# Four scheduling edits in a two-layer transformer kernel: weight loads in parts, a shared gate ring, turned steps, paced clears

## The reference, cut to what matters

```python
def body(acc, p):                       # 64 routed experts, hidden width 64 each
    W1, B1, W2, B2, e = p
    h = jax.nn.silu(xf @ W1 + B1) @ W2 + B2
    cw = jnp.sum(jnp.where(ti == e, tw, 0.0), axis=-1)
    return (acc + cw[:, None] * h, None)
...
x = x + _L0_xattn_ref(_layernorm(x), ctx, ...)
x = x + _L0_ffn_ref(_layernorm(x), ...)           # routed + shared experts
x = x + _L1_xattn_ref(_layernorm(x), ctx, ctx, mask, ...)
x = x + _L1_ffn_ref(_layernorm(x), ...)           # h = gelu(x @ bw1.T + b1) @ bw2.T + b2
```

## Time and profile before

| | us |
|---|---|
| median of 3 runs | 1317.81 (1317.72 to 1319.56) |
| profiled execution | 1319.14 |
| its span, first to last instruction | 1317.4 |
| TensorE busy | 1167.9 (89%) |
| VectorE busy | 879.4 (67%) |
| ScalarE busy | 697.0 (53%) |
| GpSimd busy | 337.8 (26%) |
| mean granted TensorE clock | 0.953 |

### The profile page before, as it was taken

How to read it: one execution, slowest core, us unless ns; L and a number is a source line. 1 busy time by engine, 2 the same in 40 slices (tenths; PEclk the granted TensorE clock), 3 DMA queues, 4 the chain that set the end, 5 groups by cost and what they waited for, 6 DMA issues and landing times. The chain is left out here.

```text
span 1317.4 us, 20464 instructions
## 1 busy us (share of the span) xinstructions
PE 1167.9 (89%) x6928; PEld 1014.4 (77%) x6928; DVE 879.4 (67%) x1669; ACT 697.0 (53%) x1053; POOL 337.8 (26%) x347
## 2 busy tenths in 40 slices
PE   3888769988879979969999999999999999978988
PEld 2666647877768969969999988778788788767877
DVE  6787765556645635635665454799999989976565
ACT  2222214655533424424444233798888988976655
POOL 2400018212123500410320025432342432332020
PEclk9888879988889989989999999999999999998999
DMA  8100001002217253252222013322421423310001
GB/s 294 64 0 0 0 8 64 1 5 68 61 48 157 65 152 96 73 144 92 93 96 89 1 40 97 102 66 73 128 64 52 139 70 103 88 38 6 14 21 48
DMA packets 66852, 92.83 MB, mean 70 GB/s; under 512 B 15440, under 2 KB 32592, under 8 KB 66640
## 3 DMA queue, kind: packets, MB, share of 16 engines
q1 hardware_dynamic: 65152, 89.67, 23.1%
q10 hardware_dynamic: 1616, 2.10, 0.5%
HBM read 80.45 MB, written 11.14 MB: 70 GB/s over the span
## 5 line engine op out<-in xcount | busy, mean ns | idle before, releaser
L1823 DVE CUSTOM_DVE_ANT_0 at_pr<-at_sc,at_mk 128x512 f32<-128x512 f32 x256 | 165.5, 684 | 24.8 <-PE at_sc L2054 24.3
L1725 ACT ACTIVATE at_pr<-at_pr,at_nmx 128x512 f32<-128x512 f32 x256 | 170.4, 716 | 21.4 <-DVE at_nmx L1823 20.7
L1969 DVE TENSOR_TENSOR W_1l<-at_pt,W_1h 128x1024 fp32r<-128x1024 f32 x128 | 155.8, 1217 | 5.5 <-ACT W_1h L1720 5.2
L2069 PE MATMUL at_pt<-ident,at_pr 128*128 128x128 f32 x1024 | 135.9, 276 | 21.1 <-DVE W_1l L1969 20.4
L2069 PEld LDWEIGHTS at_pt<-ident,at_pr 128*128 128x128 f32 x1024 | 115.5, 142 | 44.5 <-issue 25.2
L1720 ACT ACTIVATE W_1h<-at_pt 128x1024 fp32r<-128x1024 f32 x128 | 130.8, 1022 | 34.5 <-PE at_o L2088 33.1
L315 DVE TENSOR_TENSOR moe_ms<-moe_hs,moe_gate 128x512 f32<-128x512 f32 x112 | 86.2, 770 | 89.9 <-ACT moe_hs L282 56.6
L282 ACT ACTIVATE moe_hs<-moe_hid,cols 128x512 f32<-128x512 f32 x128 | 88.1, 688 | 104.0 <-PE moe_hid L167 103.0
L274 ACT ACTIVATE moe_hh<-moe_ms 128x512 fp32r<-128x512 f32 x112 | 70.8, 632 | 133.4 <-DVE moe_ms L315 133.4
L301 DVE TENSOR_TENSOR moe_hl<-moe_ms,moe_hh 128x512 fp32r<-128x512 f32 x112 | 87.9, 785 | 69.2 <-ACT moe_hh L274 69.2
L2088 PE MATMUL at_o<-W_1h,at_vaug 128*128 128x512 f32 x256 | 113.7, 444 | 0.3 <-DVE W_1l L1969 0.3
(11 more groups left out here) (314 smaller groups left out, 3293.6 us busy)
## 6 DMA issues: line engine op xcount, KB each, us to landing
moe_gate<-expert_weights SPq DMA_DIRECT2D x224, 128.0 KB, 2.9
w_stage<-in_ew SPq DMA_DIRECT2D x8, 1024.0 KB, 6.3
at_kp<-at_heads SPq DMA_DIRECT2D x96, 64.0 KB, 2.7
at_qp<-at_heads SPq DMA_DIRECT2D x96, 64.0 KB, 2.8
w_stage<-in_w SPq DMA_DIRECT2D x4, 1024.0 KB, 9.8
f_gate<-expert_weights SPq DMA_DIRECT2D x32, 128.0 KB, 2.9
w_stage<-in_mask SPq DMA_DIRECT2D x16, 256.0 KB, 3.6
at_rb<-at_recip SPq DMA_DIRECT2D x64, 64.0 KB, 2.0
```

What stands on the lines that cost most here:

```text
L1725: act.activation(pr_of(t)[:, x, :], pr_of(t)[:, x, :], ACT.Exp, bias=nmx[:, t % 4, x:x + 1], scale=-1.0).then_inc(s["ex"], 1)
L1823: dve.tensor_tensor_reduce(pr_of(t)[:, x, :], SB[x][:, :], mk[u // 2 % 2][:, j, :], -float(HD) ** -0.5, 3.0e38, ALU.add, ALU.min, nmx[:, t ...
L1969: dve.tensor_tensor(PH[1][:, n % 2, :], PT[n % 2][:, :, :].rearrange("p c q -> p (c q)"), f(PH[0][:, n % 2, :]), ALU.subtract).then_inc(s[ ...
L2069: last = pe.transpose(PT[t % 2][:, c, j * P:(j + 1) * P], pr_of(t - i + j // 2)[:, j % 2, kc * P:(kc + 1) * P], g.ident[:, :])
```

## The change

Four parts.

1. `group_dma` loads each group in eight parts of 256 KB. In `moe_phase` they are set between the gates: for q = 0 in the batch i = 3, one part behind the gates of each tile; for q = 1 and 2 in the batches i = 2 and 3, one part behind the gates of every second tile. SP's loop is written out.
2. The gate ring and its semaphores are allocated outside `front_phase` and `moe_phase` and used by both. `front_phase` issues the gates of the first four tiles of batch 2 at its end, and `moe_phase` leaves those out.
3. Last unit: TensorE's turns go to steps 3, 4, 6, 7 (they were in 3, 4, 7, 8). ScalarE's copies and VectorE's low parts of them go to steps 4, 5, 7, 8, ScalarE's ahead of L1720 and the exponentials of the step. `alphas` and `alphas2` stand behind L1969 of steps 10 and 12, not ahead.
4. GpSimd in the preparation: each pair of the clears of QP waits for one low part of the tail (`tlo`), `low_ctx` stands behind the second pair, and the clears of VAUG go in four parts, each behind a later low part and followed by one conversion of the mask.

```diff
-def group_dma(sp, g, k):
-    if k:
+PARTS = 8
+def group_dma(sp, g, k, parts=range(PARTS)):
+    if k and 0 in parts:
         sp.wait_ge(g.w_split, SPLITS * k)
...
+    for part in parts:
+        c, half = divmod(part % 4, 2)
+        if part < 4:
+            n = slice(half * H // 2, (half + 1) * H // 2)
+            sp.dma_start(first[:, c, n], g.a[name1][c * P:(c + 1) * P, at + n.start:at + n.stop]).then_inc(g.w_staged, 16)
+        else:
+            t = 2 * (part - 4)
+            sp.dma_start(second[:, t:t + 2, :],
+                         g.a[name2][at + t * P:at + (t + 2) * P, :].rearrange("(t p) n -> p t n", p=P)).then_inc(g.w_staged, 16)
 def group_split(pool, g, k):
-    pool.wait_ge(g.w_staged, 32 * (k + 1))
+    pool.wait_ge(g.w_staged, 16 * PARTS * (k + 1))
...
 # front_phase, SP, behind the last store of the expert weights
+            gates(EARLY, RING)
...
 # moe_phase, SP
             for q in range(GR):
-                first = 0 if q else EARLY
-                gates(q, first)
-                if q + 3 < GR + 2:
-                    group_dma(sp, g, q + 3)
-                with sp.Fori(first + 1, B) as i:
-                    gates(q, i)
+                for i in range(0 if q else EARLY, B):
+                    for t in range(HT):
+                        if q or i > EARLY or t >= RING:
+                            gates(q, i, t)
+                        if q + 3 < GR + 2:
+                            if q == 0 and i == B - 1:
+                                group_dma(sp, g, q + 3, range(t, t + 1))
+                            elif q and i >= B - 2 and t % 2:
+                                part = (i - B + 2) * HT // 2 + t // 2
+                                group_dma(sp, g, q + 3, range(part, part + 1))
...
 # attention_phase, GpSimd
             norm_pool(pool, nm, 0, g.power)
-            low_ctx(0)
-            clear(QP[:, :, :].rearrange("p a n -> p (a n)"), T)
+            for k in range(4):
+                pool.wait_ge(s["tlo"], k + 1)
+                clear(heads[:, 2 * k * T:2 * (k + 1) * T], T)
+                if k == 1:
+                    low_ctx(0)
             add_bias(0)
-            clear(VAUG[:, :, :, :, :].rearrange("p s t g w -> p (s t g w)"), 3 * PERIOD)
+            for k in range(4):
+                pool.wait_ge(s["tlo"], k + 6)
+                clear(places[:, 6 * PERIOD * k:6 * PERIOD * (k + 1)], 3 * PERIOD)
+                convert(0, k)
             ones()
-            for j in range(TT):
-                convert(0, j)
...
 # attention_phase, ScalarE: ahead of the copy L1720 of the step
+                    if u == UNITS - 1 and st in (4, 5, 7, 8):
+                        ffn_turn(st - 4 if st < 7 else st - 5)
...
-                    if u == UNITS - 1 and st in (3, 4, 7, 8):
-                        ffn_turn(st - 3 if st < 7 else st - 5)
...
 # VectorE
+                        if st in (4, 5, 7, 8):
+                            ffn_low_turn(st - 4 if st < 7 else st - 5)
                         if st in (2, 5):
                             ffn_apply(st // 3)
-                        if st in (3, 4, 7, 8):
-                            ffn_low_turn(st - 3 if st < 7 else st - 5)
...
 # TensorE
-                        if st in (3, 4, 7, 8):
-                            ffn_turn(st - 3 if st < 7 else st - 5)
+                        if st in (3, 4, 6, 7):
+                            ffn_turn(st - 3 if st < 6 else st - 4)
```

More of the change, by code:

```diff
@@ L189, in __init__ @@
         if gated:
-            self.gate = sb(name + "_gate", [P, RING, T], F32)
             self.ms = sb(name + "_ms", [P, RING, T], F32)
-            self.gate_loaded = [sem(f"{name}_gate_loaded{i}") for i in range(RING)]
             self.gate_used = sem(name + "_gated")
@@ L417, in build @@
                 g.cw = nc.dram_tensor("expert_weights", (E, B * T), F32).ap()
[L418 to L421 removed]
+                g.gate_loaded = [sem(f"gate_loaded{k}") for k in range(RING)]
+                with ExitStack() as st2:
+                    g.gate = maker(st2)[0]("gate", [P, RING, T], F32)
+                    with ExitStack() as st3, own_semaphores():
+                        front_phase(nc, g, *maker(st3))
+                    with ExitStack() as st3, own_semaphores():
+                        moe_phase(nc, g, *maker(st3))
             with ExitStack() as st1:
@@ L811, in front_phase @@
     s_pass = sem("dve_passed")
-    s_gate = [sem(f"fr_gate_loaded{k}") for k in range(RING)]
+    s_gate = g.gate_loaded
     s_cw = [sem(f"fr_weights_stored{k}") for k in range(2)]
@@ L832, in _, with gates @@
             group_dma(sp, g, 2)
-            def gates(b):
+            def gates(b, tiles_of_b=HT):
                 sp.wait_ge(s_cw[b % 2], 32 * (b // 2 + 1))
-                for t in range(HT):
+                for t in range(tiles_of_b):
                     n = b * HT + t
@@ L1976, in _ @@
                         ffn_step(st)
+                    if u == UNITS - 1 and st == 10:
+                        alphas()
+                    if u == UNITS - 1 and st == 12:
+                        alphas2()
                     if st == (4 if u == UNITS else 2) and u >= 1:
```

41 lines of the change are left out of this document (16 added, 25 removed).

## The result

| | before | after |
|---|---|---|
| median of 4 runs, us | 1317.76 (1315.90 to 1319.56) | 1274.91 (1273.32 to 1278.37) |
| ratio, 95% interval | | 0.9686 (0.9655 to 0.9716) |
| profiled execution, its span | 1319.14, 1317.4 | 1273.32, 1271.6 |
| mean granted TensorE clock | 0.953 | 0.971 |

42.9 us faster in the medians, 45.8 in the spans of the two profiles; forecast were 39.2. The time is inside the range and inside the likeliest case's own (1272 to 1285). The windows of the changed kernel's four stages: the expert phase from ScalarE's first `moe_hs`, attention's preparation from the tail's first matmul, units 0 to 6, unit 7. Columns as in the earlier trace rows.

The account below looks back on a forecast made before the run. Late gates in the expert phase and waits in the last attention unit were taken as the loss: 29.0 + 0.7 + 0.5 + 9.0 = 39.2 us, predicting a median of 1278.6 us; likeliest 1272 to 1285, range 1269 to 1290.

Parts of the forecast that it names:

- The three collisions: Expert phase: gates late behind weight loads; 22.6 us idle TensorE plus low clock, 29.0 us to come back whole.
- three tests of lateness: Expert phase: SP stands some 4 us; a part delays a gate 3.6 us, 8.4 free; weights land in time.
- Rival (b): Expert phase: gates still late, needing 8.4 us of delay; 1293 if half returned, 1288 with issue cost; chance 0.09.
- The ring: Expert phase's start: with gates already there VectorE starts 1.05 us earlier; 0.7 us gained, bounds 0 and 1.05.
- The pacing: Attention's preparation: moving GpSimd's work shifts contention to other work; 0.5 us gained, bounds 2.2 gain and 1.0 loss.
- The last unit: Last attention unit: step 9 starts 8.8 us earlier, `sums1` returns 1.7, ScalarE costs 1.5; 9.0 us gained, bounds 0 and 16.
- its standing at the turn before its copy and exponentials: Last unit: ScalarE needs 2.9 us against TensorE's step of some 2.5; 0.4 for each of four turns, 1.5 lost.
- Rival (a): Last unit stays as it is, by ScalarE's wait or the clock falling as before; 1287.6 us, chance 0.13.
- The first two phases: Ahead of the expert phase: loading early weights in parts taken at 0, bounds plus or minus 0.5 us.
- (c): Everything around the last unit gives: 16 us for it and all of the rest; 1270 us, chance 0.06.
- (e): The change does not do what it says, loads bunch in front of one batch; 1318 us, chance 0.02.
- Rival (d): Expert phase: slower, TensorE granted less clock under unbroken load; 0.90 eats the gain, 0.88 gives 1328; chance 0.02.

Follow-up runs that it names:

- second series: Repeat runs beside follow-up experiments: the kernel before at 1318.83 us (11 runs), the changed kernel at 1277.87 us (6 runs).
- whole_placed: Changed kernel, but groups 3 to 5 each loaded in two transfers of 1 MB where part 0 is now; 1279.41 us, ratio 0.9699.
- before_again: The kernel before, unchanged, profiled once more; 1311.91 us in one run.
- parts_only: The kernel before with only the weights of groups 3 to 5 loaded in eight parts between the gates; 1292.66 us, ratio 0.9814.
- no_pace: Changed kernel with GpSimd's preparation in its old order, unpaced; 1279.86 us, ratio 0.9702.
- after_again: The changed kernel, unaltered, run once more; 1277.87 us, ratio 0.9689.
- early_whole: Changed kernel with groups 0 to 2 loaded in two transfers each as before; 1277.45 us, ratio 0.9683.
- no_preload: Changed kernel without the gates loaded ahead of the expert phase; 1277.04 us, ratio 0.9697.
- late_ctx: Changed kernel with `low_ctx` behind the fourth low part of the tail, not the second; 1276.91 us, ratio 0.9676.

## Why the prediction was right, and where it was not

| part, by the sum | forecast | first pair | what the other profiles add |
|---|---|---|---|
| first two phases | 0 | +7.6 | spread of 375.6 to 387.8, whatever the kernel |
| parts and shared ring | 29.0 + 0.7 | +29.0 | 29.1 for the parts alone, under 0.1 for the ring |
| pacing | +0.5 | -2.1 | +2.2 to +4.0: the changed kernel's two (55.8, 56.0) against the three other old orders |
| units 0 to 6 | 0 | 0.0 | 0.0 |
| last unit | +9.0 | +11.0 | +9.5 to +13.7 over all pairs |
| behind it | 0 | +0.4 | |
| sum | 39.2 | 45.8 | 41.0 between the medians of the second series |

**The three collisions** were priced rightly at 29.0, by idle time and low clock. The three tests of lateness held: SP stands 2.8 us (forecast 4), a gate lands at the latest 5.7 us after its issue (forecast 2.9 + 3.6 = 6.5), a part lands in 4.0 us (3.6 taken), the weights are in time. Rival (b) needed 8.4 us of delay and did not come. But the 8.4 us were too many for the tile behind the load: in whole_placed its gate was issued 2.1 us late and took 4.9 us longer than usual, 7.0 us in all, and was 2.3 us late, so some 4.7 were free (an estimate from these rows). The lead there was 8.2 us, from 404.46 to 412.67, and not four tiles of 2.82. Where the prediction set part against whole by the row of the 11 us delay behind 2 MB, it read the cause too narrowly: 1.9 of those were SP standing, and what the part's place gives (gates issued ahead) counts more than its size. The expert phase near 366 us that the prediction names is 366.1, counted as in the earlier trace rows.

**The ring** was mis-sized: 0.7 forecast, under 0.1 measured. The step "with the gates there it starts 1.05 us earlier" holds, but the operation ends no earlier: it is stretched by 1.0 us. With the old ring, before_again and parts_only even reach their first output product 6.4 us behind the first matmul, where the changed kernel takes 6.55. That the cause is GpSimd's split is argued from the overlap and from an end that does not depend on the start (4.11 us in both cases), not shown by a run of its own.

**The pacing** is the step that failed, in both its bounds. "The contention goes to other work rather than away" is true of the profile of before, where the normalisations took 2.36 us and the changed kernel has TensorE wait 1.3 us longer behind the stretched low part. But that profile was the lucky one of four with the old order: 53.7 us, where the others have 58.1, 59.7 and 59.8, and what goes with it is a start of `low_ctx` 0.2 to 0.5 us later behind the first normalisation. The bound of one operation held by one of GpSimd's was wrong in kind: a normalisation was held over nine of them. Against a mean of 57.8 us in the old order, the new one's 56.0 (mean of the eight profiles with its order unchanged) gains 1.8 us; the medians of no_pace and after_again give 2.0. Neither is separated from nothing: the means rest on four profiles that spread over 6 us, the medians on ranges that overlap. What is shown is the long hold and that pacing ends it. The estimate of +0.5 has the sign of these means, by another mechanism than was argued for it, and not the sign of the first pair.

**The last unit** was walked to step 9 within 0.6 us (9.4 measured, 8.8 forecast), and `sums1` gives back 1.6 (1.7). The term that was wrong is ScalarE's: 1.5 us (0.4 for each of four turns are 1.6) were taken off for its standing at the turn before its copy and exponentials. (A low turn was also taken at 0.65 us, where the earlier trace rows gives 0.69; over four turns that is under 0.2.) Steps 4, 5, 7 and 8 take 2.95, 4.25, 3.32 and 3.14 us, where VectorE's work alone gave 3.2, 4.5, 3.1 and 3.1; ScalarE's wait does exist (up to 1.1 us in step 5), but no step is over the forecast of VectorE's work by more than 0.2 us. Up to 5.2 of the 11.0 us are clock, as said above; the walk did not price that apart. Rival (a) is refuted: the stretch is 11 us shorter, and its clock rose from 0.83 to 0.94. It did not stay at full level, though: 3.6 us at the lower one remain, beside `sums1`.

**The first two phases** were taken at 0 and showed 7.6. early_whole, with the old loads, ends them at 381.5, no_preload at 387.3, and the kernel before itself at 375.6 and 387.8: no part of the change shows in them beside that spread. So of the 45.8 us between the first two profiles some 38 are the change's; the medians say 42.9 and 41.0, with intervals of about 4 us either way, and the parts (29, 0, 2, and 11.4 between the means of the last unit) make 42. **Rivals (c) and (e)**, 1270 and 1318, lie outside what was measured. **Rival (d)** is refuted by 364 us at a clock of 1.00.

## What to carry to other kernels

A bulk load in the same queue as small urgent transfers should be issued where their ring is full and its own precondition is already met; count how long the queue stands there, since that is where lateness begins, and only then think of cutting the load up. Where two instructions of two engines that disturb each other may start in either order, one profile shows one outcome: take two or three profiles of the kernel before, and price such a stretch by its spread. A phase that no edit touches should be compared first, because its difference is the yardstick for all the others.

## What the runs showed that was not expected

TensorE's clock in the first two phases differs from run to run of one program: 0.88 and 0.93 over 340 us, and 12.2 us of time. The three runs shown ahead of the prediction agreed within 0.14%; over three later series the kernel before goes from 1308.1 to 1326.0 us.

A short operation of VectorE can be held over many of GpSimd's in a row: 5.1 us for one of 0.41, over the second half of `low_ctx` and eight clears. The Trainium skill, SBUF — State Buffer, section SBUF: two separate sides, says that GpSimd and a VectorE operation in a two-port mode, or with two inputs in that memory, share a pair of ports, and whichever of the two starts first has it for its whole instruction while the other blocks. No row names the mode of the normalisations; the third normalisation (1.4 us, one half of `low_ctx`) agrees. The fourth goes beyond it, since VectorE did not get in between GpSimd's instructions over nine of them; why not, no run here shows. The same section says that a VectorE operation with two inputs in that memory is held only by a GpSimd operation that reads it too; the low part of the weights agrees, with 2.84 us beside `low_ctx` and 1.75 beside a clear (late_ctx).
